# Experts' stage: four buffers of finished rows, and ScalarE issues the store of each pair of tiles

## What is computed

```python
xn = _layernorm(x, axis=-1)
x = x + attention(xn) + ffn(xn)
# the experts' part of ffn, 32 experts, 6 chosen for each token, width 96:
g = jnp.einsum('td,edf->tef', x, wg)
u = jnp.einsum('td,edf->tef', x, wu)
act = jax.nn.silu(g) * u
routed = jnp.einsum('tef,efd,te->td', act, wd, combine)
```

## Time and profile before

| | us |
|---|---|
| median of 3 runs | 1435.52 |
| the runs | 1435.43 to 1436.6 |
| the profiled execution | 1436.87 |
| its span | 1434.7 |
| TensorE busy (PE) | 1302.8, 91% |
| VectorE busy (DVE) | 938.8, 65% |
| ScalarE busy (ACT) | 851.0, 59% |
| GpSimd busy (POOL) | 588.7, 41% |
| experts' stage, from start to end | 611.5 to 959.7 |

### The profile page before, as it was taken

The page is one execution under the profiler, slowest core; times in us unless marked ns, Lnnn a source line. Parts: engine busy times, 40 slices in busy tenths (PEclk is TensorE's granted clock), DMA queues, the critical chain, the costliest instruction groups (busy, mean ns, idle before and its releaser), DMA issues. The chain is left out here.

```text
span 1434.7 us, 24478 instructions
## 1 busy us (share of the span) xinstructions
PE 1302.8 (91%) x7385; PEld 963.7 (67%) x7385; DVE 938.8 (65%) x3727; ACT 851.0 (59%) x2294; POOL 588.7 (41%) x607
## 2 busy tenths in 40 slices
PE   4899769999999999889999999988899898998996
PEld 3566446777776777677888888865566666666664
DVE  3578678777777777423664333327888888888784
ACT  1455437677666667445566666646666666666663
POOL 1111127776676777400000000014666666566663
PEclk8899979999999999999999999989999999999998
DMA  9776652323228222298855555532233332332321
GB/s 345 309 266 249 247 201 96 111 82 107 100 82 301 103 96 78 70 286 310 268 179 177 177 176 179 177 121 70 85 101 85 103 107 78 107 107 78 107 74 56
DMA packets 133844, 216.98 MB, mean 151 GB/s; under 512 B 14743, under 2 KB 108631, under 8 KB 128855
## 3 DMA queue, kind: packets, MB, share of 16 engines
q1 hardware_dynamic: 101462, 152.48, 31.2%
q0 software_dynamic: 18432, 50.36, 10.8%
q10 hardware_dynamic: 13824, 12.59, 2.8%
HBM read 103.70 MB, written 111.67 MB: 150 GB/s over the span
## 5 line engine op out<-in xcount | busy, mean ns | idle before, releaser
L1708 ACT ACTIVATE l_prob<-l_prob,l_negmax 128x512 f32<-128x512 f32 (+3 forms) x256 | 142.1, 556 | 154.3 <-DVE l_negmax L1794 154.2
L1063 POOL DMA_INDIRECT sorted_x<-f_xn_row,slot_no x192 | 204.5, 1065 | 49.9 <-issue 49.3
L1219 ACT ACTIVATE f_prob<-f_prob,f_negmax 128x512 f32<-128x512 f32 (+3 forms) x256 | 142.6, 558 | 122.0 <-DVE f_negmax L1292 120.0
L1601 PE MATMUL ps<-l_kt,l_qt 128*128 128x512 f32 (+3 forms) x512 | 176.9, 452 | 39.1 <-DVE l_qt L1772 22.4
L1539 POOL DMA_INDIRECT l_rows<-sorted_y,slot_no x192 | 185.6, 967 | 49.1 <-issue 41.6
L2126 DVE TENSOR_TENSOR act_f<-hidden,ps 128x96 f32<-128x96 f32 x224 | 56.9, 254 | 211.1 <-ACT hidden L2101 210.3
L2063 PE MATMUL ps<-wgu_sb,xt_e 128*128 x896 | 185.0, 329 | 7.5 <-ACT xt_e L2096 7.5
L1122 PE MATMUL ps<-kt_s,f_qt 128*128 128x512 f32 (+3 forms) x512 | 170.4, 447 | 5.7 <-DVE f_qt L1283 4.4
L1292 DVE CUSTOM_DVE_ANT_0 f_prob<-ps,mask_add 128x512 f32<-128x512 f32 (+3 forms) x256 | 121.0, 486 | 81.0 <-issue 80.1
L1794 DVE CUSTOM_DVE_ANT_0 l_prob<-ps,mask_add 128x512 f32<-128x512 f32 (+3 forms) x256 | 122.0, 485 | 71.8 <-issue 70.6
L2063 PEld LDWEIGHTS ps<-wgu_sb,xt_e 128*128 128x128 f32 x896 | 141.0, 191 | 10.1 <-issue 9.9
(11 more groups left out here) (202 smaller groups left out, 2940.1 us busy)
## 6 DMA issues: line engine op xcount, KB each, us to landing
sorted_x<-zeros SPq DMA_DIRECT2D x14, 2048.0 KB, 8.9
rows_in<-sorted_x SPq DMA_DIRECT2D x112, 256.0 KB, 3.0
sorted_y<-rows_out SPq DMA_DIRECT2D x112, 256.0 KB, 2.1
wgu_sb<-in_wgu SPq DMA_DIRECT2D x16, 384.0 KB, 5.3
x_in<-in_x SPq DMA_DIRECT2D x8, 512.0 KB, 9.7
xn_dram<-xn SPq DMA_DIRECT2D x8, 512.0 KB, 3.7
base_dram<-x_in SPq DMA_DIRECT2D x8, 512.0 KB, 2.9
nqt_dram<-nqt_out SPq DMA_DIRECT2D x8, 512.0 KB, 3.9
```

The lines of the kernel that those rows point to most:

```text
L1063: pool.indirect_dma_start(sorted_x, bass.IndirectOffsetOnAxis(ap=slot_no[:, t, k:k + 1], axis=0), xn_row[buf][:], None).then_inc(scattered ...
L1219: act.activation(prob[:, i, qt, 0:w], prob[:, i, qt, 0:w], ACT.Exp, bias=negmax[:, i, qt:qt + 1], scale=-1.0, accum_out=rowsum[:, g // 2 % ...
L1601: mm = pe.matmul(s_ps[k % 2][:, 0:w], qt[g // 2 % 2][g % 2][:, n * P:w], kt[b - HB][:, 0:w], start=True, stop=True)
L1708: act.activation(prob[:, i, qt, 0:w], prob[:, i, qt, 0:w], ACT.Exp, bias=negmax[:, i, qt:qt + 1], scale=-1.0, accum_out=rowsum[:, g // 2 % ...
```

## The change

`rows_out` has four buffers, allocated behind the other tiles of the stage, and four semaphores `out_stored`. The two memsets that raised these semaphores are gone, and with them the tile `primer_b`; ScalarE waits for a buffer only from the fifth pair on. SyncE no longer issues the stores: ScalarE waits for its own copy of a pair's second tile and issues the store itself, before it goes on with the next tile's `xt_e` copy. Before its first copy it waits for `done.res_stored`.

```diff
-    rows_out = [sb(f"rows_out{i}", [P, 2, H]) for i in range(2)]
+    OUT = 4
...
+    rows_out = [sb(f"rows_out{i}", [P, 2, H]) for i in range(OUT)]
-    primer = sb("primer_b", [P, 4])
...
-            def store(r, par):
-                sp.wait_ge(y_copied, 2 * r + 2)
-                sp.dma_start(out_pairs[r], rows_out[par][:]).then_inc(out_stored[par], 16)
...
-                    if not (isinstance(i, int) and r < 2):
-                        store(r - 2, d % 2)
...
-            for par in range(2):
-                sp.wait_ge(out_stored[par], 16 + 16 * (NTILE // 4))
+            for o in range(OUT):
+                sp.wait_ge(out_stored[o], 16 * (NTILE // 2 // OUT))
...
-                        d = (j - 3) // 2
+                        r = c // 2
                         act.wait_ge(y_ready, c + 1)
-                        if par == 1:
-
-                            act.wait_ge(out_stored[d % 2], 16 * (PAIRS // 2 * i + d // 2) + 16)
-                        act.activation(rows_out[d % 2][:, (j - 3) % 2, :], y_ps[1 - par], ACT.Copy)\
+                        if c % 2 == 0 and r >= OUT:
+
+                            act.wait_ge(out_stored[r % OUT], 16 * (r // OUT))
+                        if c == 0:
+                            act.wait_ge(done.res_stored, 16 * HB + 16)
+                        act.activation(rows_out[r % OUT][:, c % 2, :], y_ps[1 - par], ACT.Copy)\
                            .then_inc(y_copied, 1)
+                        if c % 2 == 1:
+                            act.wait_ge(y_copied, c + 1)
+                            act.dma_start(out_pairs[r], rows_out[r % OUT][:]).then_inc(out_stored[r % OUT], 16)
...
-            for par in range(2):
-                dve.memset(primer[:, par:par + 1], 0.0).then_inc(out_stored[par], 16)
```

More of the change, by code:

```diff
@@ L1972, in sorted_tiles @@
     y_ps = [ps[:, 6 + i, 0:H] for i in range(2)]
-    out_stored = [sem(f"rows_stored{i}") for i in range(2)]
+    out_stored = [sem(f"rows_stored{i}") for i in range(OUT)]
     xt_ready, xt_copied = sem("ext_ready"), sem("ext_copied")
@@ L2015, in body @@
                         load(r + AHEAD - 1, (d + AHEAD - 1) % AHEAD)
-                    if not (isinstance(i, int) and r < 2):
-                        store(r - 2, d % 2)
             iterations(sp, body)
-            for r in range(NTILE // 2 - 2, NTILE // 2):
-                store(r, r % 2)
-            for par in range(2):
-                sp.wait_ge(out_stored[par], 16 + 16 * (NTILE // 4))
+            for o in range(OUT):
+                sp.wait_ge(out_stored[o], 16 * (NTILE // 2 // OUT))
         @block.tensor
```

## The result

The changed kernel takes 1476.56 us (median of 4 runs, 1473.29 to 1481.36) beside 1436.06 us for the kernel before on the same chip: a ratio of 1.0275, 95% interval 1.0248 to 1.0302. That is 40.5 us slower, against a forecast of 3.5 us slower and outside the range. Lines move with the change: `xt_e` is L2088 after it, `hidden` L2093, `rows_out` L2103, ScalarE's issue L2107; TensorE's turn of a tile L2044, gate and up L2055, the turn of the activated tile L2065, down L2073; the read of the expert numbers L2029.

What follows compares the result with a forecast made beforehand. Transfers pace two early stretches of the experts' stage, TensorE the long rest; -2.5 - 2.8 us of early gains + 8.8 us (98 cycles x 0.09) = +3.5 us, so 1439.0 us, range 1429.5 to 1448.

Steps and rivals of the forecast that it cites:

- ScalarE's terms: Between odd rows_out copy and next xt_e copy: 0.41 us to issue, 0.36 issue, 0.04 behind it; 0.81 instead of 0.28.
- Rival C: ScalarE's store issue is dearer or has a 0.2 us tail: 0.26 us a cycle, 1455.7 us; chance 0.15 with all between.
- The term of 2.11 us: Experts' stage: late xt_e copy's start to next odd rows_out copy, 2.11 us; with 0.81 a 2.92 us cycle against 2.83.
- the same 0.09 on top of 3.03: Cycles of two tiles where TensorE reads expert numbers: assumed to pay 0.09 us more, like the other cycles.
- rival D: Expert-number read runs on while TensorE waits, so 49 read cycles pay nothing: 1434.6 us, no change; chance 0.13.
- The slack of 0.44 us: Room between xt_e copy's end and TensorE's weights: 0.44 us left, against 0.53 us of delay.
- rival B: ScalarE's issue hides, cycle stays 2.83 us, only early gains remain: 1430.2 us, or 1428.0; chance 0.22.
- Part 2: Four buffers and another queue: ScalarE's 11.4 us of store waits go, gaining 2.5 and 2.8 us in two early stretches.
- a rate of 306 GB/s: First early stretch, from 611 us: transfers at 306 GB/s pace the stage, so tile 26 can start at 655.9 us.
- the end that I left aside, 4.7: First early stretch: upper end of the buffers' gain, 4.7 us, to count where bytes don't bind; 2.5 was taken.
- the 660 that I had put down as a sign against part 2: Thirteenth odd rows_out copy, expected near 658.3 us; at 656 or 660 the early-gain forecast would be wrong.
- wrong in part 1 if the cycles from 700 us are over 3.0: Sign against the forecast for ScalarE issuing stores: two-tile cycles still 2.83 or over 3.0 us, where 2.92 was expected.

Runs made afterwards that it cites:

- e10: Changed kernel with expert weights at a fixed address (experts' outputs wrong) and the expert numbers not read at all: 1414.40 us.
- e3: Changed kernel's four buffers, but SyncE issues the stores as before; ScalarE only waits for its own odd copy before the next xt_e copy: 1435.30 us.
- e5: Changed kernel, with ScalarE's issue at the same place but storing the previous pair, whose copies ended long ago: 1429.53 us.
- e2: Changed kernel's four buffers kept, the stores put back on SyncE at their old places: 1430.41 us.
- e9: Changed kernel with expert weights of L2055 and L2073 at a fixed address (experts' outputs wrong), expert numbers still read: 1443.03 us.

## Why the prediction was wrong

- **ScalarE's terms were right.** 0.41 to the issue, 0.36 for it (112 times 0.365 to 0.383), 0.04 behind it, 0.81 in sum: measured 0.41, 0.37, 0.04 and 0.83. Rival C, the dearer issue, didn't come.
- **The term of 2.11 us was mis-sized**, because it came from one tile. The copy at 629.37 is moreover not the next odd one but that of the even tile 6; it stands to the late tile as the odd copy does in the changed kernel, so the relation carries over. At the earlier trace rows the late tile is the first of its four, whose number needs one register operation less, as the view of L2063 from 627.5 to 627.95 us shows for the kernel before:

```profile
L2063 PEldq ALU_OP  x2: 36/36/36, 627.7 to 627.9; - x2
```

  The weights follow the copy's end by 0.23 us there, and by 0.33 to 0.37 in the tiles that are late in the changed kernel, with three such operations (above). Of the second stalled case of before, with three operations, I had taken no row; it has 0.37 us (676.40 to 676.77):

```profile
676.02 0.38 ACT L2096 ACTIVATE xt_e<-ps 128x256 f32<-128x256 f32 x1
...
676.77 0.62 PEld L2063 LDWEIGHTS ps<-wgu_sb,xt_e 128*128 128x128 f32 x4 [0.99 <-issue]
```

  From the start of `xt_e` to the next odd copy it is 2.25 in the cycle shown (821.63 to 823.88) and 2.21 in the median of the cycles without a read, so with 0.83 the cycle is 3.04 and not 2.92, and costs 0.20 and not 0.09. Over 55 cycles that is 11 us.
- **The step that failed was the read cycles'**: "the same 0.09 on top of 3.03". They grew by 0.73 us (3.06 to 3.78, before rounding 3.055 to 3.783), 40 us over 55 cycles. Of that 0.20 is the arithmetic, as in the others, and 0.53 is the read ending later: 0.35 because it starts later, the rest because it takes 0.78 us and not 0.59, and the cause of this rest, some 10 of the 40 us, is open. I treated the 0.2 us of the read as a fixed cost beside the wait, and my bound, rival D, went the other way: that a waiting TensorE could read meanwhile. The read stands behind the matmuls in TensorE's program and so behind the same wait; delayed matmuls delay it. Its start against its step's weights, 793.1 to 793.32, wasn't in my rows, and it is what told that the read was hidden by a lead of the sequencer which the change takes away.
- **The slack of 0.44 us** in rival B was 0.67 less a reaction of 0.23, and the reaction was that of the tile with one operation less. For the tiles that are late it is 0.67 - 0.33 = 0.34, and the delay of 0.55 passes it by 0.21, which is the 0.20 measured; with a fixed address it is 0.67 - 0.12 = 0.55, and the same delay just fits (e10). The delay of 0.14 in e3 and e5 fits in cycles without a read. Rival B named the right quantity; its size depends on the register work.
- **Part 2** held in kind: no ScalarE wait for a stored buffer is left. Its size was 4.8 + 2.4 = 7.2 us in e2's cycles where I had 2.5 + 2.8. The first was cut by a rate of 306 GB/s taken for a ceiling, and e2 moved 333; the end that I left aside, 4.7, was the right one. In the changed kernel little of it shows, 41.27 us for twelve cycles against 40.96, since cycles of 3.04 and 3.8 fill that time. The thirteenth odd copy came at 663.92, past the 660 that I had put down as a sign against part 2; 2.8 us of it is the later start of the stage.
- The sum by what was measured: 55 x 0.20 + 55 x 0.73 = 51.2, less some 9 of stalls gone early (91.91 us for the first 28 cycles of before, where 28 unstalled ones are 82.5), about 42 against 40.0 between the odd copies.
- My own signs caught it: "wrong in part 1 if the cycles from 700 us are over 3.0", and the expected wait at L2063 for `xt_e` doesn't appear; the profile calls it "issue", because the sequencer has the wait.

## What to carry to other kernels

Ask of every semaphore wait which instruction carries it: a register instruction or a value read behind a late wait runs in the open, even where the engine itself has slack; put address work and reads ahead of the wait. Moving an issue to the engine that makes the data puts its wait for itself and the issue in series in front of whatever that engine does next; storing the previous pair, or issuing behind the urgent copy, avoids it. Take a reaction time from a case of the same kind as the one that is to be costed, and look at more than one.

## What was not expected of the hardware

- A value read by TensorE's sequencer takes 0.30 us ahead of the wait for the data and, in the medians of the kernels, 0.52 to 0.97 us right behind the gate and up matmuls, but 0.30 there too in some stretches; why is open. The Trainium skill's "DMA: Bandwidth & Descriptors", "Latency and other measured facts", gives about 600 ns as the floor of a `tensor_load`; the trace has 295 ns for its TENSOR_LOAD, so here it doesn't hold.
- From the end of a copy to the weights that wait for it: 0.12 us with a fixed address, 0.33 us with a register address (medians of the late tiles, e9 and after).
- ScalarE waiting for its own last copy starts the next one 0.42 us behind it instead of 0.28, 0.14 us more, and an issue without that wait costs the same 0.14 us, since it runs beside the copy.
